# First attention of a transformer kernel: each head's last 13 context tokens packed in 16 rows instead of 32

## What is computed

```python
q = einsum('bsd,hdk->bhsk', layernorm(x), wq) + bq        # 16 heads of 64
k = einsum('bsd,hdk->bhsk', ctx, wk) + bk
v = einsum('bsd,hdv->bhsv', ctx, wv) + bv
attn = softmax(where(mask, q @ k.T / 8, -1e9))            # over 77 context tokens
x = x + tanh(g_xattn[0]) * (einsum('bhst,bhtv->bhsv', attn, v).reshape(...) @ wo + bo)
```

## Time and profile before

| what | value |
|---|---|
| median of 3 runs | 742.88 us (742.69 to 750.19) |
| the profiled execution, whole | 743.47 us |
| its span, first to last instruction | 741.6 us |
| TensorE busy | 610.3 us (82% of the span) |
| VectorE, ScalarE, GpSimd busy | 450.0, 321.1, 216.0 us |
| mean granted TensorE clock | 0.905 of full speed |
| first `short_keys` (ahead of the loop) | starts at 33.60 us |
| last matmul of tile 15's `attend` | ends at about 230.4 us |

### The profile page before, as it was taken

One profiled execution on the slowest core, in us unless ns is written; L12 is line 12 of the kernel. 1 busy time (PEld: TensorE's weight loads), 2 busy tenths in 40 slices (PEclk: granted clock), 3 DMA queues, 4 the chain that ended last, 5 costly groups with the idle time before them and its releaser, 6 DMA issues.

```text
span 741.6 us, 14125 instructions
## 1 busy us (share of the span) xinstructions
PE 610.3 (82%) x5391; PEld 409.7 (55%) x5391; DVE 450.0 (61%) x1243; ACT 321.1 (43%) x698; POOL 216.0 (29%) x407
## 2 busy tenths in 40 slices
PE   4999999999995797553788899988888888846687
PEld 4576666666654585421455555555565555524674
DVE  3576768777775115779983565447656667275552
ACT  2453544445333242434431322206657677713164
POOL 2124242453444246300211405412523411020400
PEclk9999999999997798657697699999979999977898
DMA  8770000000002152000001132122030300030001
GB/s 257 187 233 1 1 1 1 1 16 1 8 8 76 47 167 80 0 1 0 0 1 35 29 89 64 36 57 64 6 96 5 98 6 7 4 114 1 3 0 58
DMA packets 33604, 34.51 MB, mean 47 GB/s; under 512 B 8730, under 2 KB 29506, under 8 KB 32962
## 3 DMA queue, kind: packets, MB, share of 16 engines
q1 hardware_dynamic: 31072, 31.02, 14.7%
q0 software_dynamic: 1024, 2.11, 0.8%
q10 hardware_dynamic: 1442, 0.48, 0.3%
HBM read 19.63 MB, written 5.26 MB: 34 GB/s over the span
## 4 chain that ended last, share of the span: by engine, by line
PE 62%; DVE 16%; issue 10%; ACT 4%; POOL 4%; DMA 3%; POOLq 0%; SPq 0%; DVEq 0%; ACTq 0%
PE bank L592 6%; PE bank L1676 6%; PE bank L1926 5%; PE bank L517 4%; PE bank L548 4%; PE bank L526 4%; PE bank L1941 3%; PE bank L1730 3%; PE bank L560 2%; PE bank L1974 2%; PE bank L2355 2%; PE bank L535 2%; DVE mx L2077 2%; POOL y_tokens L1224 2%; PE bank L446 2%
## 5 line engine op out<-in xcount | busy, mean ns | idle before, releaser
L2077 DVE TENSOR_REDUCE mx<-bank 128x4 f32<-128x512 f32 (+1 forms) x128 | 71.0, 581 | 40.4 <-PE bank L1934 40.1
L2145 ACT ACTIVATE area_a<-bank 128x512 f32<-128x512 f32 (+1 forms) x128 | 73.7, 597 | 38.4 <-PE bank L1941 37.0
L943 ACT ACTIVATE area_a<-bank,beta 128x154 f32<-128x154 f32 x128 | 41.9, 412 | 76.3 <-PE bank L517 76.0
L592 PEld LDWEIGHTS bank<-area_a 128*128 128x128 f32 x384 | 48.2, 196 | 24.7 <-issue 15.0
L1031 POOL TENSOR_TENSOR area_a<-area_a,rs 128x512 f32<-128x512 f32 (+1 forms) x48 | 40.9, 879 | 48.8 <-DVE rs L751 48.8
L592 PE MATMUL bank<-area_a 128*128 128x128 f32 x384 | 55.0, 288 | 0.0
L1676 PE MATMUL bank<-area_a 128*128 128x512 f32 x80 | 42.8, 663 | 0.9 <-DVE X L1624 0.9
L548 PE MATMUL bank<-area_a,xnT 128*128 128x512 f32 (+1 forms) x96 | 41.6, 515 | 0.0
L517 PE MATMUL bank<-ctx_flat,area_a 128*128 128x154 f32 x256 | 41.6, 296 | 0.0
L1264 POOL TENSOR_TENSOR g_veps<-g_mv,eps 128x4 f32<-128x4 f32 x20 | 4.0, 202 | 128.1 <-DVE g_mv L1259 128.1
L517 PEld LDWEIGHTS bank<-ctx_flat,area_a 128*128 128x128 f32 x256 | 36.4, 190 | 7.9 <-issue 7.1
(11 more groups left out here) (358 smaller groups left out, 1479.7 us busy)
## 6 DMA issues: line engine op xcount, KB each, us to landing
area_a<-xn_area SPq DMA_DIRECT2D x48, 128.0 KB, 2.5
area_b<-in_w SPq DMA_DIRECT2D x16, 256.0 KB
f<-in_f SPq DMA_DIRECT2D x1, 2048.0 KB
area_a<-in_f SPq DMA_DIRECT2D x1, 2048.0 KB, 8.5
area_b<-xn_area SPq DMA_DIRECT2D x6, 308.0 KB, 5.6
area_a<-in_rows SPq DMA_DIRECT2D x10, 128.0 KB, 2.8
x_slots<-xn_area SPq DMA_DIRECT2D x1, 1032.0 KB, 8.0
area_a<-x_slots SPq DMA_DIRECT2D x8, 129.0 KB
```

The source lines that it names most:

```text
L592: m = pe.matmul(WO, eT0[:, i, :], vv0[:, b % 2, i, :], start=(i == 0), stop=(i == 11))
L943: m = act.activation(kk0[:, g % 2, h, :], src[:, (h - lo) * 2 * T:(h - lo + 1) * 2 * T], ACT.Identity, bias=beta0[:, h:h + 1])
L2077: dve.tensor_reduce(mx3[:, b % 2, aux, heads3(half, 1 - odd)], SCORES_RING3[j % 2][:, 0:4 * n].rearrange("p (h k) -> p h k", k=n), AX.X, A ...
L2145: act.activation((ea3 if aux else em3)[:, heads3(half, odd), :], EXP_RING3[j % 2][0:T if aux else 128, :].rearrange("p (h q) -> p h q", q= ...
```

## The change

Each head's 13 short tokens stand in 16 rows where they had 32. Eight heads then fill 128 rows, and the short part has 2 operands where it had 4; a tile has 10 operands where it had 12.

TensorE's output can be placed only at rows 0, 32, 64 and 96, so two heads now share a block of 32 rows. `short_keys` does that with two accumulating matmuls per block. A new array `ends0` holds, for each sample, 16 columns of zeros, the 13 short tokens, and zeros up to 48 columns. Its slice 16:48 puts the tokens in the first 16 rows of the block and zeros in the rest; its slice 0:32 puts zeros first and the tokens in the last 16 rows. The first (k = 0) starts the sum, the second (k = 1) adds to it.

```diff
-        vv0 = carve("A", (at0, (2, 12, D)), 128)
+        vv0 = carve("A", (at0, (2, 10, D)), 128)
...
-        es0 = carve("A", (at0, (2, H0, TP - 64)), 128)
-        eT0 = carve("A", (at0, (12, 128)), 128)
+        es0 = carve("A", (at0, (2, H0, 16)), 128)
+        eT0 = carve("A", (at0, (10, 128)), 128)
+        ends0 = carve("A", (at0, (B, 48)), 128)
...
-                for r in range(4):
-                    m = pe.matmul(dst[32 * r:32 * r + 32, :], ctx_flat[:, b * T + 64:b * T + TP], wvo0[:, r:H0:4, :],
-                                  start=True, stop=True)
+                for k in range(2):
+                    for r in range(4):
+                        m = pe.matmul(dst[32 * r:32 * r + 32, 0:2 * D], ends0[:, b, 16 - 16 * k:48 - 16 * k], wvo0[:, 2 * r + k:H0:8, :],
+                                      start=(k == 0), stop=(k == 1))
...
-                for i in range(4):
-                    part = el0[:, b % 2, 8 * c + 2 * i:8 * c + 2 * i + 2, :] if c < 2 else es0[:, b % 2, 4 * i:4 * i + 4, :]
+                for i in range(4 if c < 2 else 2):
+                    part = el0[:, b % 2, 8 * c + 2 * i:8 * c + 2 * i + 2, :] if c < 2 else es0[:, b % 2, 8 * i:8 * i + 8, :]
...
-                for i in range(4 * c, 4 * c + 4):
-                    m = pe.matmul(WO, eT0[:, i, :], vv0[:, b % 2, i, :], start=(i == 0), stop=(i == 11))
+                for i in range(4 * c, min(4 * c + 4, 10)):
+                    m = pe.matmul(WO, eT0[:, i, :], vv0[:, b % 2, i, :], start=(i == 0), stop=(i == 9))
...
+            pe.wait_ge(route0_loaded, 8 * 16)
             short_keys(0)
-            pe.wait_ge(route0_loaded, 7 * 16)
...
-                dve.tensor_copy(flat(vv0[:, b % 2, 4 * n + 4:4 * n + 8, :]), ring0_bank("vd", 2 * b + n)[:, :]).then_inc(vv_dve_done, 1)
+                i = 4 if n == 0 else 2
+                dve.tensor_copy(flat(vv0[:, b % 2, 4 * n + 4:4 * n + 4 + i, :]), ring0_bank("vd", 2 * b + n)[:, 0:i * D]).then_inc(vv_dve_done, 1)
...
-                act.activation(flat(eT0[:, 4 * c:4 * c + 4, :]), T0[c % 2][:, :], ACT.Copy).then_inc(turn_done, 1)
+                i = 4 if c < 2 else 2
+                act.activation(flat(eT0[:, 4 * c:4 * c + i, :]), T0[c % 2][:, 0:i * 128], ACT.Copy).then_inc(turn_done, 1)
...
-            pool.memset(es0[:, :, :, T - 64:TP - 64], 0.0).then_inc(pool_ready, 1)
+            pool.memset(es0[:, :, :, T - 64:16], 0.0).then_inc(pool_ready, 1)
...
             sp.dma_start(X[:, 2:B, :], t["x"][:, 2:B, :]).then_inc(x_loaded, 16)
+            sp.dma_start(ends0, t["ends0"]).then_inc(route0_loaded, 16)
```

More of the change, by code:

```diff
@@ L116, in build @@
         kk0 = carve("A", (at0, (2, H0, 2 * T)), 128)
-        at_wv, at_wq = [at0[0]], [at0[0] + 2 * 12 * D]
-        vv0 = carve("A", (at0, (2, 12, D)), 128)
+        at_wv, at_wq = [at0[0]], [at0[0] + 2 * 10 * D]
+        vv0 = carve("A", (at0, (2, 10, D)), 128)
         el0 = carve("A", (at0, (2, H0, 64)), 128)
-        es0 = carve("A", (at0, (2, H0, TP - 64)), 128)
-        eT0 = carve("A", (at0, (12, 128)), 128)
+        es0 = carve("A", (at0, (2, H0, 16)), 128)
+        eT0 = carve("A", (at0, (10, 128)), 128)
+        ends0 = carve("A", (at0, (B, 48)), 128)
         wv0 = carve("A", (at_wv, (8, D)), 128)
@@ L864, in vector_attn0 @@
             dve.wait_ge(x_loaded, 16)
-            dve.wait_ge(route0_loaded, 7 * 16)
+            dve.wait_ge(route0_loaded, 8 * 16)
             for b in range(B):
@@ L2647 @@
         "ctxT": np.concatenate([a["ctx_1024"].transpose(2, 0, 1).reshape(D, B * T), np.zeros((D, 32), np.float32)], axis=1),
+        "ends0": np.pad(a["ctx_1024"].transpose(2, 0, 1)[:, :, 64:], ((0, 0), (0, 0), (16, 48 - 16 - (T - 64)))),
         "mask": a["mask_BxSxS2_bk1"].transpose(1, 0, 2),
```

## The result

The changed kernel takes 740.28 us in the median of 9 runs (734.46 to 743.37), the kernel before 744.9 us in the median of 9 beside it (742.69 to 754.9): a ratio of 0.9899, 95% interval 0.9852 to 0.9945. It is faster, by 4.6 us, about half of the forecast 9.8, and the 740.28 us lie outside the range of 731.0 to 736.7. The profiled execution took 740.1 us with a span of 738.1, against 743.47 and 741.6. Medians here are over all runs of a kernel, ratios and their intervals only over the fast ones, those within 1.5% of its fastest run.

A forecast was written before the change was run, and what follows sets the result against it. TensorE was taken as the bound in tiles 0 to 12 of the first attention; 13 tiles x 0.655 + 3 x 0.435 = 9.82 us off 743.47 gives 733.65, less 0.59 for the median: 733.1 us, range 731.0 to 736.7.

The forecast's parts named there:

- Two transposes: Third `turn` group of each first-attention tile: 4 transposes become 2, saving 0.22 us a tile on TensorE.
- four matmuls: Third `attend` group of each first-attention tile: 8 matmuls become 4, saving 0.445 us a tile on TensorE.
- the new `short_keys`: 16 matmuls of 256 columns replace 8 of 512; the group costs 0 to 0.05 us more, taken as 0.01.
- Tiles 8, 13 and 14: First-attention tiles where TensorE waits for VectorE at `turn_norms`: the transposes' 0.22 us is lost, leaving 0.435 us each.
- Rivals 1: In `short_keys`, weight loads stand bare: +0.22 us in each of 16 tiles, gain 6.3, time 736.6; chance 0.07.
- Rivals 1 and 2: The second: accumulating `short_keys` matmuls do not run side by side; 30 us slower, 773 us; chance 0.03.
- Rival 3: First attention: VectorE's chain becomes the bound, `turn_norms` waits in every tile; gain 7.2, time 735.7; chance 0.07.
- The operations costed at nothing: VectorE's and ScalarE's copies, the memset, the `ends0` load and TensorE's moved wait for loads: each forecast at 0.
- I leave it as it is: Tile 15's granted clock, averaging 0.79, was kept unchanged in the forecast, since the wait ahead keeps its length.
- rival 4: Tile 15's half-clock stretch goes, 1.6 us more gain, 731.5, or another comes, 734.7; chance 0.06.
- The text's own test: If the span outside 20 to 235 us changes by more than 1 us, the account is wrong somewhere.
- the start, costed at 0: Ahead of the first `short_keys`: the new 384 KB load of `ends0` and TensorE's moved wait add 0.

The follow-up runs named there:

- run 2: The changed kernel, unedited, measured again in a later sitting: 751.02 us (12 runs), ratio 0.9845 to the kernel before.
- run 3: The changed kernel with the load of `ends0` moved behind the issue of area_b's load: 751.34 us, ratio 0.9946.
- run 10: The changed kernel with GpSimd's mask conversion made to wait for VectorE's second `xn`: 747.25 us, ratio 0.9966.
- run 5: The changed kernel with 5 unused 512-column matmuls ahead of the last attention's loop: 740.74 us (6 runs), ratio 0.9845.
- run 6: The kernel before with 12 unused 512-column matmuls ahead of the last attention's loop: 755.12 us, ratio 1.003.
- run 12: The changed kernel with GpSimd's mask conversion held for the second `xn` and 16 unused matmuls in the last attention's first two tiles: 738.77 us, ratio 0.9839.
- run 8: The kernel before with 16 unused 512-column matmuls in the last attention's first two tiles: 749.44 us, ratio 0.999.
- run 11: The kernel before with GpSimd's mask conversion held for the second `xn` and 16 unused matmuls in the last attention's first two tiles: 749.35 us, ratio 0.9965.
- run 9: The kernel before with GpSimd's mask conversion made to wait for VectorE's second `xn`: 754.19 us (6 runs), no ratio on record.

## Why the prediction was wrong

The part that was worked out came true term by term. Two transposes gave 0.21 us (0.22), four matmuls 0.45 (0.445), the new `short_keys` cost 0.01 (0.01). Tiles 8, 13 and 14 gave 0.45, 0.44 and 0.37 (0.435 each), the others 0.66. Tile 12 is 12.02 us. Rivals 1 and 2 are out: the group of 1.01 us is below both 1.2 and 1.67, and 16 loads lie within its matmuls. By the rule of the Trainium skill quoted in the prediction (loads overlap only with matmuls of another row group) it would have been longer; the trace goes against the rule. Rival 3 is out, as tile 12 has no gap. The operations costed at nothing hid as expected, VectorE's and ScalarE's copies among them.

The step that failed is the clock: "I leave it as it is", and with it the subtraction 743.47 - 9.82, which takes every stage behind the loop as a constant. The page had warned, in the slices of its clock (5 to 7 tenths in several slices behind the loop) and in tile 15's 0.79, but I looked for a clock effect only where the change's own instructions run, and put 1.6 us and a chance of 0.06 on it. In tile 15 the forecast of rival 4 came true in the first pair of profiles (2.24 us less where 0.66 was due), by chance: the stretch is in tile 15 of the changed kernel again in runs 2, 3 and 10, and of the eight profiles with the long loop only the first has it. Far behind it, in the last attention, the shorter loop costs 6 to 12 us: 175.8 to 176.1 us where the long loop has 164.3 to 169.7. Between the loop and that stage it gives some us back, 7.7 in the first pair. The text's own test, that more than 1 us outside 20 to 235 us would mean an error somewhere not looked at, found exactly this.

The second term is the start, costed at 0. It was +2.91 us in the pair of profiles, mostly chance: 22.88 us was the earliest of 16 starts.

The third is the base. 742.88 us was the median of 3 runs; with 9 it was 744.9, and in four later sittings 751.6 to 753.3. Of the 7.2 us by which 740.28 missed 733.1, 2.0 are the base and 5.2 the smaller gain. A range 5.7 us wide around one such number was narrower than the kernel's own scatter of 742 to 762 us. Had I carried that scatter and the clock of the later stages as terms, the range would have reached past 740.

Not settled: why the shorter loop puts TensorE's idle time in the last attention so that the clock falls there. Five more matmuls ahead of it undid it in the one profile with them (run 5), so where the work stands in time seems to matter and not what it is; that is argued, not shown. Twelve in the kernel before did not bring it (run 6). Nor is it settled which of the later stretches, such as one of 58 us from 639 us on in run 10, come with what.

## What to carry to other kernels

Where a profile shows the clock at half level in stages behind the one that is changed, their length is not a constant: carry each such stage's spread over repeated profiles as a term of its own before the range is drawn. Compare runs at equal half-clock time as well as by their medians; that tells a real saving from what the clock gave or took. Then look at where the clock falls, since 16 matmuls of no use at that place gave nearly as much here (10 us in the stage, 8.5 in the median of run 12 against run 10) as the change itself. In the kernel before, without the long stretch, they gave some 2 to 3 us in the median (runs 8 and 11), within the scatter.

## What the runs showed of the hardware

- A saving early in a program brought a stretch at half clock (23.9 us long) into a stage some 270 us behind it, in five of five profiles with the short loop that are neither filled nor shifted, and in none of the eight with the long one.
- One us more at half clock goes with 0.28 to 0.29 us more run time in two groups of runs (12 of run 2, 93 of the kernel before; 0.22 in the first nine of the changed kernel), and not with the 0.5 by which work that takes twice as long would lengthen it. That waits make the difference is argued, not shown. The Trainium skill, "TensorE: Matmul & The Clock Gate" (Terms), puts the penalty at the time below full clock times one less the ratio, so 0.5; these runs stay below it.
- The first clock entry of run 9 is at 21.7 us, and windows ahead of it print 1.00 while durations are doubled. The same page of the Trainium skill (Part 1, the caveats on its trace events) says such events should not be trusted one by one; the trace agrees, with 3.22 us against 1.74.
- A VectorE instruction of 0.35 us took 1.35 to 1.39 where GpSimd's of 1.22 us is on record as beginning 0.05 to 0.09 us behind it (six of 16 profiles), and 0.35 in all others, the four that keep them apart among them; in run 2 GpSimd's began 0.14 us behind and took 1.28 itself. The Trainium skill, "SBUF — State Buffer" (SBUF: two separate sides), says that GpSimd and VectorE, in certain of its instructions, lock one port pair against each other for a whole instruction, and that the first to start gets it; the trace agrees with the lock, except that here the one on record as first was the one held up.
